# A decoder on one core: the second layer's key/value side made smaller and moved to the last three head pairs, the eight head-masked key copies moved from ScalarE to GpSimd

## The reference, cut to what matters

```python
kh = _split_heads(_layernorm(k @ wk, ln_gamma, ln_beta))      # k = v = ctx_1024
vh = _split_heads(_layernorm(v @ wv, ln_gamma, ln_beta))
k_prime = (jax.nn.relu(kh) + EPS_K) * em                      # em: the mask, one number per key row
vh = vh * em
kv = jnp.einsum('bhnd,bhne->bhde', k_prime, vh)
z = 1.0 / (jnp.einsum('bhnd,bhd->bhn', q_prime, k_prime.sum(axis=-2)) + EPS_K)
```

## Time and profile before

| what | us |
|---|---|
| median of three runs | 1208.59 |
| the profiled execution, its own time | 1209.53 |
| its span (first to last instruction) | 1207.7 |
| TensorE busy | 991.9 |
| VectorE busy | 686.5 |
| ScalarE busy | 520.4 |
| GpSimd busy | 484.0 |
| start of pair 0 of batch 0 / 5 / 6 / 7 | 86.3 / 591.4 / 692.8 / 792.8 |

### The profile page before, as it was taken

How to read it: one execution, slowest core, us unless ns; L and a number is a source line. 1 busy time by engine, 2 the same in 40 slices (tenths; PEclk the granted TensorE clock), 3 DMA queues, 4 the chain that set the end, 5 groups by cost and what they waited for, 6 DMA issues and landing times.

```text
span 1207.7 us, 19775 instructions
## 1 busy us (share of the span) xinstructions
PE 991.9 (82%) x7491; PEld 664.9 (55%) x7491; DVE 686.5 (57%) x1895; ACT 520.4 (43%) x1414; POOL 484.0 (40%) x553
## 2 busy tenths in 40 slices
PE   4578899899799979989979998998746999996311
PEld 3355566566566656656756665665434755663311
DVE  2535666566656666666765767654474002445498
ACT  3726545564664465556466446532211233331000
POOL 1224555546455554654645555465421000111031
PEclk8779899799999989989998999999956999997655
DMA  6000000000000000000000000000000000010401
GB/s 167 18 3 13 1 1 14 1 1 6 10 1 1 14 2 1 14 1 1 6 10 1 1 1 1 1 19 1 1 1 1 2 1 4 8 8 3 52 0 35
DMA packets 56813, 12.85 MB, mean 11 GB/s; under 512 B 40318, under 2 KB 56462, under 8 KB 56590
## 3 DMA queue, kind: packets, MB, share of 16 engines
q1 hardware_dynamic: 56718, 11.58, 4.7%
HBM read 9.46 MB, written 2.12 MB: 10 GB/s over the span
## 4 chain that ended last, share of the span: by engine, by line
PE 58%; DVE 23%; ACT 10%; POOL 3%; issue 3%; DMA 2%; SPq 1%; POOLq 0%; DVEq 0%
PE score_banks L1572 8%; PE out_bank L1544 8%; PE bank_d L1670 6%; PE bank_a L1339 5%; DVE o_rec L1050 5%; PE score_banks L1734 4%; PE score_banks L1358 4%; DVE prob L1078 3%; ACT prob L716 3%; PE score_banks L1383 3%; DVE stats L885 3%; PE out_bank L1527 3%; PE score_banks L1360 2%; PE score_banks L1359 2%; PE out_bank L1552 2%
## 5 line engine op out<-in xcount | busy, mean ns | idle before, releaser
L776 ACT ACTIVATE prob<-score_banks 128x1024 f32<-128x1024 f32 x128 | 130.8, 1022 | 154.5 <-PE score_banks L1572 154.1
L1572 PE MATMUL score_banks<-qh,kr 64*128 64x256 f32 x1024 | 153.2, 420 | 6.2 <-ACT prob L776 4.9
L616 POOL TENSOR_TENSOR psum<-psum,prob 128x512 f32<-128x512 f32 x64 | 81.6, 1274 | 166.1 <-DVE prob L1078 166.1
L539 POOL TENSOR_TENSOR var_eps<-mv,epsilons 128x2 f32<-128x2 f32 (+2 forms) x64 | 12.6, 197 | 335.6 <-DVE mv L888 335.4
L1050 DVE RECIPROCAL o_rec<-out_bank 128x256 f32<-128x256 f32 x64 | 111.8, 1747 | 32.9 <-PE out_bank L1552 32.9
L1544 PE MATMUL out_bank<-prob,v 128*64 128x256 f32 x1024 | 124.6, 385 | 1.3 <-DVE on L1051 1.3
L614 POOL TENSOR_TENSOR psum<-prob 128x512 f32<-128x512 f32 x64 | 82.3, 1286 | 99.5 <-DVE prob L1078 99.5
L1572 PEld LDWEIGHTS score_banks<-qh,kr 64*128 64x128 f32 x1024 | 92.8, 195 | 45.4 <-issue 26.6
L1078 DVE TENSOR_SCALAR prob<-prob 128x1024 f32<-128x1024 f32 x128 | 101.2, 790 | 26.9 <-ACT prob L776 26.9
L1010 DVE TENSOR_TENSOR k_cos<-score_banks,cos_t 128x512 f32<-128x512 f32 x56 | 38.6, 690 | 123.0 <-POOL kr L590 75.4
L716 ACT ACTIVATE prob<-prob,neg_max 128x128 f32<-128x128 f32 (+1 forms) x256 | 106.4, 420 | 0.0
(11 more groups left out here) (352 smaller groups left out, 2035.6 us busy)
## 6 DMA issues: line engine op xcount, KB each, us to landing
cb<-in_ctx_dram SPq DMA_DIRECT2D x8, 256.0 KB, 2.9
bias_mask<-bias_scratch SPq DMA_DIRECT2D x1, 1536.0 KB, 7.5
xb<-in_x_dram SPq DMA_DIRECT2D x8, 128.0 KB, 2.2
prob<-in_L_xattn_Wkv_dram SPq DMA_DIRECT2D x1, 1024.0 KB, 6.8
att_scratch<-on SPq DMA_DIRECT2D x16, 64.0 KB, 3.1
prob<-att_scratch SPq DMA_DIRECT2D x2, 512.0 KB, 4.1
out_dram<-v SPq DMA_DIRECT2D x4, 256.0 KB, 2.3
prob<-in_L_xattn_Wq_dram SPq DMA_DIRECT2D x1, 512.0 KB, 8.1
```

Of the source, the lines that this page charges most:

```text
L616: link(g.tensor_tensor(psum[:, p % 2, :], psum[:, p % 2, :], pp[:, 2, :], ALU.add))
L776: s.activation(prob[:, p % 2, 2 * u:2 * u + 2, :].rearrange("p k (h q) -> p h k q", h=2), sc[:, 0:2, :].rearrange("p h (k q) -> p h k q", ...
L1572: last = mm(sc[:, h, k * T:(k + 1) * T], kr[rows_of, p % 2, kb * P:(kb + 1) * P], qh[rows_of, p % 2, :], start=True, stop=True, skip_group ...
```

## The change

It does four things.

1. Weights of the second layer's keys and values are centred once in the preamble (each row's mean is taken off), so that the products have mean zero and only a scale is needed. The multiplication by gamma and the addition of beta for the values move behind the sums (two VectorE instructions on 128x128); the mask multiplies the scale and two extra columns of `v1`; the affine of the keys stays, 128x512 twice on GpSimd.
2. The copy to `kv1` goes: VectorE measures the product in `bank_a`, ScalarE scales it from there into `k1` and `v1`, and only then is the bank free.
3. The context is turned in slot 34; products in slots 35 and 39, scales on GpSimd in 36 and 40, scaled copies by ScalarE in 37 and 41, the affine in 42 and 43, the rectifier in 44, the sums in 47 (before: slots 3 to 23 and 40).
4. The eight masked copies are made by GpSimd as `tensor_scalar`, in the same slots 3 to 6.

```diff
-S_CTX_NORM, S_NORM, S_KV_NORM, S_AFFINE, S_RELU = 5, (9, 13), (10, 15), (17, 18, 19, 20), 23
-S_SUMS, S_REC, S_DIVIDE, S_PROJ, S_X1, S_LATN, S_KV, S_LAT = 29, 33, 34, 35, 37, 38, 40, 43
+S_CTX_NORM = 5
+S_SUMS, S_REC, S_DIVIDE, S_PROJ, S_X1, S_LATN, S_LAT = 29, 33, 34, 35, 37, 38, 43
+S_TURN_CTX, S_KV, S_KV_SCALE, S_KV_OUT = 34, (35, 39), (36, 40), (37, 41)
+S_AFFINE, S_RELU, S_KV_SUM = (42, 43), 44, 47
...
@@ gpsimd
+                if slot in S_MASKED:
+                    if slot == S_MASKED[0]:
+                        pool.wait_ge(a_free, n(b, ACT_JOBS, SETUP_A + A_K + 1))
...
+                    at = 2 * S_MASKED.index(slot)
+                    for jj in HEAD_PAIRS[at:at + 2]:
+                        g.tensor_scalar(km[:, jj, :], k0[:, :], mask_of_8[:, jj:jj + 1], 1.0, ALU.mult,
+                                        ALU.mult).then_inc(km_ready, 1)
+                if slot in S_KV_SCALE:
+                    half = S_KV_SCALE.index(slot)
+                    scale = act_scale[:, 1 + half, :]
...
+                        g.tensor_copy(v1[:, :, D:D + 2], keep_pair[:, b, :, :])
+                    pool.wait_ge(kv_var_ready, n(b, 2, half + 1))
+                    link(g.tensor_tensor(var_eps[:, 4:8], mv[:, 4:8, 1], epsilons[:, EPSILONS.index(1e-6), 4:8], ALU.add))
+                    link(g.tensor_tensor(scale, var_eps[:, 4:8], minus_half[:, 4:8], ALU.pow))
+                    g.tensor_tensor(scale, scale,
+                                    kv_factor[:, b, 2 * half:2 * half + 2, :].rearrange("p k t -> p (k t)"),
+                                    ALU.mult).then_inc(kv_scale_ready, 1)
                 if slot in S_AFFINE:
...
+                    first = slot == S_AFFINE[0]
+                    if first:
+                        pool.wait_ge(a_free, n(b, ACT_JOBS, SETUP_A + A_KV + 2))
+                    row, op = (l1_g, ALU.mult) if first else (l1_b, ALU.add)
+                    last = g.tensor_tensor(k1[:, :, :], k1[:, :, :], row[:, :].unsqueeze(1).broadcast_to([P, KB, D]), op)
...
@@ scalar
+                if slot in S_KV_OUT:
+                    half = S_KV_OUT.index(slot)
+                    act.wait_ge(kv_scale_ready, n(b, 2, half + 1))
...
+                    for i in range(4):
+                        dst = (k1[:, 2 * half + i // 2, :], v1[:, 2 * half + i // 2, 0:D])[i % 2]
+                        last = s.activation(dst, bank_a[:, i * D:(i + 1) * D], ACT.Identity,
+                                            scale=act_scale[:, 1 + half, i:i + 1])
+                    last.then_inc(a_free, 1)
-                if slot in S_MASKED:
...
-                        s.activation(km[:, jj, :], k0[:, :], ACT.Identity,
-                                     scale=mask_of_8[:, jj:jj + 1]).then_inc(km_ready, 1)
...
@@ vector
+                if slot in S_KV:
+
+                    half = S_KV.index(slot)
+                    dve.wait_ge(a_full, n(b, ACT_JOBS, SETUP_A + A_KV + half + 1))
+                    if half == 1:
+                        dve.wait_ge(kv_scale_ready, n(b, 2, 1))
+                    measure(tiles_of(bank_a[:, :].rearrange("p (k d) -> p k d", d=D), 4), 1, kv_var_ready)
                 if slot == S_RELU:
                     dve.wait_ge(kv_ready, n(b, 1, 1))
...
-                    link(w.tensor_scalar(k1[:, :, :], kv1_v[:, :, 0, :], 0.0, 1e-6, ALU.max, ALU.add))
-                    w.tensor_tensor(v1[:, :, 0:D], kv1_v[:, :, 1, :], keep_b, ALU.mult)
-                    w.tensor_tensor(k1[:, :, :], k1[:, :, :], keep_b, ALU.mult).then_inc(k1_ready, 1)
+                    w.tensor_scalar(k1[:, :, :], k1[:, :, :], 0.0, 1e-6, ALU.max, ALU.add).then_inc(k1_ready, 1)
...
@@ tensor
-                if slot == S_CTX:
+                if slot == S_TURN_CTX:
...
-                if slot in (S_KV_A, S_KV_B):
-                    j = slot - S_KV_A
+                if slot in S_KV:
+                    j = S_KV.index(slot)
...
-                if slot == S_KV:
+                if slot == S_KV_SUM:
 
                     bank = d_job(D_KV)
                     pe.wait_ge(k1_ready, n(b, 1, 1))
```

More of the change, by code:

```diff
@@ L58 @@
 SLOTS = PER_PAIR * PAIRS
-S_X, S_K, S_Q, S_CTX, S_V, S_KV_A, S_KV_B = range(7)
+S_X, S_K, S_Q, S_CTX, S_V = range(5)
 S_CN = 7
@@ L542, in rstd_of, with scale_and_bias @@
                                 ALU.pow).then_inc(done, 1)
[L544 to L548, removed]
+            def scale_and_bias(before):
+                scale, bias = act_scale[:, 0, :], act_bias[:, :]
+                pool.wait_ge(var_ready, before + 1)
+                link(g.tensor_tensor(var_eps[:, 4:8], mv[:, 4:8, 1], epsilons[:, 0, 4:8], ALU.add))
                 link(g.tensor_tensor(scale, var_eps[:, 4:8], minus_half[:, 4:8], ALU.pow))
@@ L561, in self_attention @@
                 if slot == S_CTX:
-                    scale_and_bias(norms, 0, EPS_LN)
-                if slot in S_NORM:
-                    scale_and_bias(norms, 1 + S_NORM.index(slot), 1e-6)
-                if slot in S_AFFINE:
[L567 to L573, removed]
+                    scale_and_bias(norms)
@@ L672, in evacuate, with apply_norm @@
                     i.then_inc(a_free, 1)
-            def apply_norm(norms, k, dst, src):
-                act.wait_ge(rstd_ready, norms + k + 1)
-                for i in range(4):
-                    last = s.activation(dst[:, i, :], src[:, i, :], ACT.Identity, scale=act_scale[:, k, i:i + 1],
-                                        bias=act_bias[:, k, i:i + 1])
+            def apply_norm(norms):
+                act.wait_ge(rstd_ready, norms + 1)
+                for i in range(KB):
+                    last = s.activation(cn[:, i, :], cb[:, i, :], ACT.Identity, scale=act_scale[:, 0, i:i + 1],
+                                        bias=act_bias[:, i:i + 1])
                 return last
@@ L875, in _ @@
             w.tensor_copy(cos_t[:, :], bank_d[:, :]).then_inc(d_free, 1)
+            for half in range(2):
+                w.bn_stats(stats[:, half, :], w_l1kv[:, half * D:(half + 1) * D])
+            link(w.memset(stats[:, 2, 0:1], 0.0))
+            for half in range(2):
+                w.bn_aggr(mv[:, half, :], stats[:, half, :])
+            link(w.memset(stats[:, 2, 0:1], 0.0))
+            for half in range(2):
+                tile = w_l1kv[:, half * D:(half + 1) * D]
+                last = w.tensor_scalar(tile, tile, mv[:, half, 0:1], None, ALU.subtract)
+            last.then_inc(kv_centred, 1)
             def band_of(h, count):
@@ L1463, in self_attention @@
                     for kb in range(KB):
[L1464 removed]
+                        last = mm(bank[:, 0:D + 2], k1[:, kb, :], v1[:, kb, :], start=(kb == 0), stop=(kb == KB - 1))
                     last.then_inc(d_full, 1)
```

86 lines of the change are left out of this document (43 added, 43 removed).

## The result

The changed kernel is slower: 1225.82 us (1224.28 to 1227.05) against 1209.18 (1207.61 to 1209.96) for the kernel before, ratio 1.014 with a 95% interval of 1.013 to 1.016. Its profiled execution took 1225.5 us.

What follows compares the result with a forecast made beforehand. TensorE's own work was taken to bound most pairs, key/value stalls pairs 1 and 2. Seven batches at +1.8 (+12.6) and the preamble (+8.9) gave 1231.0, about 1230 us; forecast 1213 to 1243 (0.60), range 1190 to 1250.

Steps and rivals of the forecast that it cites:

- Pair 2: Pair 2 of each batch: without the key/value norms no wait over 0.5 us, 11.7 instead of 20.0, so -8.3.
- Pairs 0 and 1: Pairs 0 and 1: less TensorE work and no `cn_s` wait, against masked copies delaying GpSimd's inverse deviation; -0.45, bounds -1.6 and +1.5.
- Pair 5: Pair 5: the context's turn and first product arrive where TensorE is full, with 0.2 of a wait; +1.6.
- pair 6: Pair 6: four scaled copies (1.65) make ScalarE 1.0 late for `exps(1)`, delaying the queries' copy; +0.35.
- Pair 7: Pair 7: late second half of the key/value side delays the exponent and the sums, plus slow clock; +9.05 us.
- the clock's 1.9: Pair 7: two TensorE idle times of about 3 us lower its clock; +1.9 a batch, bounds 0 and 3.0.
- The exponent's 3.75: Pair 7: scaled copies ahead of the first exponent on ScalarE delay the second unit to 692.2; +3.75 a batch.
- the wait's 2.7: Pair 7, slot 47: TensorE waits 2.7 for the keys' rectifier before the sums; with their 1.05 of matmuls, +3.75.
- The preamble: Before batch 0: two norms leave ScalarE's chain (-3.1), the new key/value chain lies open (+12.0); together +8.9.
- A: Rival, chance 0.16: key/value chain fits under pairs 6 and 7, first exponent of pair 7 on time; faster, 1174.
- B: Rival, chance 0.12: same stalls, but no slow clock and half the wait at slot 47; about equal, 1207.
- C: Rival, chance 0.12: masked copies over 0.6 each on GpSimd, blocked clamps, lower clock in pair 1; slower, 1251.

Runs made afterwards that it cites:

- the fastest kernel: Changed kernel with masked copies on ScalarE, the key/value product's second half in bank_d, and the sums' matmuls behind the next batch's first unit: 1171.78 us.
- the run with half of the copies: Changed kernel with the first four masked copies (slots 3 and 4) on ScalarE, the last four still on GpSimd: 1222.83 us, ratio 1.012.
- the run with the other bank: Changed kernel with masked copies on ScalarE and the key/value product's second half in bank_d, slot 36, its scale and scaled copies earlier: 1211.19 us, ratio 1.002.

## Why the prediction was right, and where its steps were off

The direction, the range and the sum held: 1231.0 for this execution by the sum, 1225.5 measured. That a batch came out at +1.6 against +1.8 is luck: against the averages over the seven batches pair 2 was priced 2.3 us too low and pair 7 2.1 too high, and the two cancel. Pair 2, pair 7, the preamble and the last part carry the differences.

- **Pair 2 (-8.3 predicted, -6.5 measured).** The norms' stalls went as told. But behind the two idle times in pair 1, of which there is only one with the copies on ScalarE, the first unit of pair 2 runs at the low clock (2.08 instead of 1.13; stretch clock 0.91). I had put 1 us of clock into a rival and none into the sum. With the copies on ScalarE pair 2 takes 12.3, still 0.6 above the 11.7 that I had found. There the reading was off: 14.1 less 3.0 is 11.1 and not 11.3, and part of the low clock had fallen into idle time, so neither is TensorE's work. In the fastest kernel that work is 11.69 in pair 2 at a granted clock of 1.00, so 11.7 left no room for any wait.
- **Pairs 0 and 1 (-0.45 predicted, 0.0 measured).** The mechanism was right line by line: VectorE goes on 17.45 after the pair's start (17.25 predicted), the copies take 0.47 to 0.49 each (0.42), the wait for `cn_s` is gone, two instructions are blocked for 0.7. What I didn't see is what this equality hides: without the copies pairs 0 and 1 would have been 2.7 shorter, with 1.1 more in pair 2. I bounded the copies by their own price and blocking, 1.6 below and 1.5 above, while two runs give 22 and 26 us (3.2 and 3.7 a batch). It did not harm the sum, since it priced the state with the copies in.
- **Pair 5, pair 6.** +1.6 and +1.7 agree. In pair 6 the four scaled copies, read from PSUM, start 0.25 apart and take 1.1 together, not the 1.65 taken from the earlier trace rows; the +0.35 is 0.
- **Pair 7 (+9.05 predicted, +6.7 measured, +7.0 on average).** The second unit was told to start 8.05 after the first, and it did. The rectifier was told to end at 13.25, and it ran from 13.0 to 13.45. The step that failed is the clock's 1.9: it was added to a wait that VectorE ends. Slow work ahead of that wait only shortens it (1.24 instead of 2.7). Without this term the sum gives 16.1 for the pair, where 15.7 was measured. The rows of other batches bear this out: in six of the seven batches of the kernel after the second unit takes between 1.43 and 2.08, and the pair takes 15.7 in each of them. In three batches of the run with half of the copies it takes 1.14, the wait is 1.6, and the pair takes 15.7 again:

```profile
389.62 1.14 PE L1617 MATMUL score_banks<-qh,kr 64*128 64x256 f32 x8 [0.47 <-ACT prob L807]
395.18 1.13 PE L1509 MATMUL bank_d<-v,k 128*128 128x130 f32 x8 [1.64 <-DVE k L1001]
```

  The term is paid where the low clock lasts beyond the wait: in batch 4 the sums take 2.07 instead of 1.13 and the pair 17.5. The exponent's 3.75 and the wait's 2.7 are two stretches of one chain. Their sum was right within 0.4, but neither comes back when it alone is taken away: with the exponent early the pair was no shorter. The end of the chain, 13.25 and then 1.05 for the sums and 1.2 for what follows, gives 15.5.
- **The preamble (+8.9 predicted, +6.8 measured).** In the chain that ended last, the reciprocals' turn and the first key product:

```profile
63.78 0.38 PE bank_a L1371 x2
...
84.29 2.07 PE bank_d L1498 x8
86.36 0.43 PE score_banks L1390
```

  The distance is 22.6 us where I had worked out 22.4. The part ahead of that turn, from which the two norms went, is 4.3 shorter instead of 3.1 (68.04 in the earlier trace rows against 63.78 here; that the norms alone made it so is not shown), and from the first key product to the first unit it takes 6.7 instead of 7.9.
- The last part, 1.9 shorter, was not predicted. Of it 1.15 lie in pair 0 of batch 7, which takes 10.4 instead of 11.6: in the kernel before TensorE waits there for VectorE's division, and in the kernel after it doesn't.

```profile
800.59 3.84 PE L1527 MATMUL out_bank<-wo,on 128*128 128x128 f32 x32 [1.16 <-DVE on L1051]
```

  The rest isn't explained; over all kernels here the last part lies between 413.0 and 417.3 us.

Of the rivals, A named the right deciding point in pair 7 but the wrong remedy: statistics right behind the product (the run with the other bank) weren't enough, because GpSimd and VectorE come last there. Its 1174 was reached only with the sums out of the way and the copies back on ScalarE. B's two conditions can be found in pair 7, half the wait (1.24) and a slow clock that costs nothing, but not its time: they would give 14.8 for the pair. The wait was halved because slow work filled it, and not because VectorE was earlier. C's mechanism, blocked instructions and a lower clock by the masks, was there at a copy of 0.47, below the 0.6 from which I let it decide.

## What to carry to other kernels

Price a chain by when it ends, not by the waits along it: idle times that the same late result ends are one cost, and slow clock ahead of such a wait is inside it, while slow clock that lasts beyond it is paid in full. Before an operation moves to another engine for nothing, name the wait that covers it and ask whether another edit of the same change removes that wait. Where a chain can't be shortened, move what is queued behind its wait; here that was worth 3%, but only once the waits ahead of it had gone.

## What the runs showed of the hardware

- GpSimd holds up VectorE's work between SBUF tiles also where that work has a single tensor input: the rectifier on 128x512 takes 0.42, and 1.49 beside a GpSimd sum; `normalize_output` 0.97 beside two masked copies, 0.60 free. With two inputs, `lat_s` takes 1.45 beside an affine and 0.41 free (in the run with the earlier rectifier). GpSimd's own instructions get longer too (one affine 1.59, the other 1.28). The reciprocal, which reads PSUM, took 1.72 to 1.76 in the kernel after, beside GpSimd's work or not. The Trainium skill, "VectorE: DVE Perf Modes", "Why PSUM operands drop a tier", says that VectorE's mode with two SBUF read ports is closed to an operand in PSUM, for which it has only one; that the reciprocal is not held up fits that. It names no size of the delay.
- Two masked copies of 128x256 took GpSimd 0.94 and ScalarE 0.89.
- The same idle time on TensorE can be followed by either level of the clock. With the masks on ScalarE one of 2.10 left the next eight matmuls at 0.82 in batches 3 to 6; with the exponent first one of 2.08 was followed by 1.44 in five batches. Idle times of 2.72 and 0.48 were followed by a second unit of 1.43 to 2.08 in the kernel after, but of 1.14 in two batches of the run with the earlier rectifier. One unbroken of 3.4 or more in front of the sums left them, or the work right behind them, at the low level in every batch. What decides between the levels wasn't settled, and neither was what tells the 17.5 of pair 7 from the 15.7.
